# A decoder layer on one core: some transposes moved from TensorE to DMA, and element work shifted between VectorE, ScalarE and GpSimd

## What is computed

```python
x = x + attn(layernorm(x))     # 16 query heads in 4 groups, 4 key heads, rope, causal softmax, y @ Wo + bo
x = x + xattn(layernorm(x), ctx, mask)   # scores = x @ ctx.T / 16, masked softmax, readout = attn @ ctx
x = x + ffn(layernorm(x))

def ffn(x):                    # I = 704
    xq, w1q = q(x), q(w_gate_up)         # q: v / (max|v| / 127) rounded to integers, times the scale, per row
    gate, up = split(xq @ w1q.T, I)
    hq, w2q = q(silu(gate) * up), q(w_down)
    return hq @ w2q.T
```

## Time and profile before

| | us |
|---|---|
| Median of three runs | 102.81 |
| The three runs | 101.42, 102.81, 103.00 |
| The profiled execution, its own time | 101.47 |
| Its span, first to last instruction | 99.80 |
| Outside the span | 1.67 |
| Busy in the span: PE, DVE, POOL, ACT | 90.2, 75.7, 66.1, 65.7 |

### The profile page before, as it was taken

The page is one execution under the profiler, slowest core; times in us unless marked ns, Lnnn a source line. Parts: engine busy times, 40 slices in busy tenths (PEclk is TensorE's granted clock), DMA queues, the critical chain, the costliest instruction groups (busy, mean ns, idle before and its releaser), DMA issues.

```text
span 99.8 us, 2432 instructions
## 1 busy us (share of the span) xinstructions
PE 90.2 (90%) x804; PEld 68.8 (69%) x804; DVE 75.7 (76%) x217; ACT 65.7 (66%) x175; POOL 66.1 (66%) x136
## 2 busy tenths in 40 slices
PE   5999699999889999989999999979999999999560
PEld 4698467977576676767776777768778887775220
DVE  5046979957998988877896659797977788988731
ACT  1404216938839886776597878969986996988410
POOL 6266847975787977914638788848868962892220
PEclk9999999999999999999999999999999999999995
DMA  2999999940000000000000000000000010012121
GB/s 36 346 337 415 419 407 409 360 143 3 3 0 7 0 3 0 7 0 0 0 7 0 0 0 0 3 7 0 0 0 0 0 56 7 0 59 99 55 103 53
DMA packets 4521, 8.34 MB, mean 84 GB/s; under 512 B 349, under 2 KB 3358, under 8 KB 4382
## 3 DMA queue, kind: packets, MB, share of 16 engines
q1 hardware_dynamic: 4272, 7.96, 21.7%
q10 hardware_dynamic: 238, 0.23, 0.9%
HBM read 7.15 MB, written 1.05 MB: 82 GB/s over the span
## 4 chain that ended last, share of the span: by engine, by line
PE 72%; DVE 10%; POOL 7%; issue 5%; ACT 3%; DVEq 0%; POOLq 0%; ACTq 0%
PE ps_s L443 14%; PE ps_r L262 6%; PE ps_q L303 6%; PE ps_y L525 4%; PE ps_r L289 4%; PE ps_r L386 3%; PE ps_x L375 3%; PE ps_s L339 3%; PE ps_y L351 3%; PE ps_y L359 3%; PE ps_q L311 2%; PE ps_x L365 2%; DVE rot L846 2%; PE ps_s L469 2%; PE ps_y L354 2%
## 5 line engine op out<-in xcount | busy, mean ns | idle before, releaser
L1156 POOL TENSOR_TENSOR gate_up<-gate,up_row 128x704 f32<-128x704 f32 x7 | 11.9, 1698 | 3.7 <-ACT gate L723 3.5
L262 PE MATMUL ps_r<-warm 128*128 128x256 bf16 x60 | 9.4, 317 | 1.1 <-DVE warm L771 1.1
L262 PEld LDWEIGHTS ps_r<-warm 128*128 128x128 bf16 x60 | 6.7, 115 | 3.0 <-DVE warm L771 1.1
L1125 POOL TENSOR_TENSOR rot_c<-rot,b_rope 128x128 f32<-128x128 f32 x8 | 3.7, 459 | 7.5 <-DVE rot L846 7.5
L869 DVE RECIPROCAL y_rsum<-ps_y 128x128 f32<-128x128 f32 x8 | 7.6, 951 | 1.1 <-PE ps_y L354 1.0
L443 PE MATMUL ps_s<-gate_hi,x_int_T 128*128 128x352 f32 x28 | 7.5, 350 | 0.0
L1187 POOL TENSOR_TENSOR y_out<-ffn,x_aug 128x256 f32<-128x256 f32 x7 | 5.1, 729 | 3.7 <-DVE ffn L1025 3.7
L525 PE MATMUL ps_y<-w_T,h_T 128*128 128x256 bf16 (+1 forms) x42 | 6.5, 276 | 0.9 <-DVE ffn L1025 0.8
L443 PE MATMUL ps_s<-up_int,x_int_T 128*128 128x352 f32 x32 | 6.9, 337 | 0.0
L443 PE MATMUL ps_s<-gate_lo,x_int_T 128*128 128x352 f32 x28 | 6.8, 323 | 0.0
L610 ACT ACTIVATE p_self_T<-ps_s 128x512 f32<-128x512 f32 x8 | 4.8, 597 | 2.4 <-PE ps_s L339 2.4
(11 more groups left out here) (194 smaller groups left out, 285.8 us busy)
## 6 DMA issues: line engine op xcount, KB each, us to landing
ctxT<-in_ctxT SPq DMA_DIRECT2D x1, 1024.0 KB, 8.6
w_raw<-in_w SPq DMA_DIRECT2D x2, 512.0 KB, 11.0
ctx_aug<-in_ctx SPq DMA_DIRECT2D x1, 1024.0 KB, 17.0
out_x<-y_out SPq DMA_DIRECT2D x8, 128.0 KB, 1.7
x_aug<-in_x SPq DMA_DIRECT2D x1, 768.0 KB, 6.8
xT<-in_xT SPq DMA_DIRECT2D x1, 768.0 KB, 9.8
w_raw<-in_w SPq DMA_DIRECT2D x1, 704.0 KB, 14.6
x_first<-in_x_first SPq DMA_DIRECT2D x1, 416.0 KB, 4.3
```

The lines of the kernel that those rows point to most:

```text
L262: nc.tensor.matmul(ps_r[:, 0:2 * T], warm[:, 0:P], warm[:, :], start=True, stop=True)
L1156: nc.gpsimd.tensor_tensor(gate_up[j % 2][:, :, :], gate[j % 2][:, :, :], up_row[:, :].rearrange("p (i f) -> p i f", i=2), ALU.mult).then_i ...
```

## The change

- The up half of w1 (int16), w2 and h of batches 0 to 5 are transposed by DMAs from SP's queue, from SBUF to SBUF. For w2 and h, DVE first copies the int16 values to bf16 (`widen_w2`, `widen_h`) into buffers of 768 columns laid over w1_raw. The PE transposes and evacuations for them are gone; up_int is still written by ACT, now from up_T in SBUF. h of batches 6 and 7 goes through PE as before.
- The row scales of w1 and w2 are transposed once on PE (13 rows), copied, stored to DRAM by one DMA and read back into all partitions by a second; up_row and w2_row are views of the result.
- `scale_down` of batches 0 to 5: ACT multiplies by h_scale (`scale_down_rows`), then POOL multiplies by w2_row (`weigh_down`). Batches 6 and 7 stay on DVE.
- `rotate_sum` moves from DVE to POOL, all eight batches, same operation.
- EARLY = 3: batch 2 takes tanh too.
- The lists of all engines are written anew. PE's list has 61 keep_warm matmuls. SP's queue holds, behind the loads: the up transpose, the scale store and reload, two w2 transposes, then the transposes of h and the stores as listed.

The diff, cut (the removed helpers are those named above):

```diff
+    BY_DMA = 6
+    SPLIT = 6
...
-    EARLY = 2
+    EARLY = 3
...
+        w1_flat = w1_raw[:, :, :].rearrange("p o d -> p (o d)")
+        UT = (WT - GT) * DC * P // 2
+        up_T = w1_flat[:, 0:UT].bitcast(I16).rearrange("p (o c t) -> p o c t", c=DC, t=P)
+        padded = w1_flat[:, UT:UT + 2 * FC * P].bitcast(BF16).rearrange("p (i f) -> p i f", f=FC * P)
+        w2_bf = padded[:, 0:DC]
+        h_bf = [padded[:, DC + i] for i in range(2)]
...
+            done(sp, "w1_int_ready", 4)
+            sp.dma_start_transpose(up_T[:, :, :, :].rearrange("p o c t -> p (o c) t"),
+                                   w1_int[:, GT:WT, :].rearrange("p o d -> p (o d)")).then_inc(s["up_T_loaded"], 16)
+            done(sp, "scale_rows_ready", 0)
+            sp.dma_start(scale_rows_dram, scale_rows[:, :]).then_inc(s["scale_rows_stored"], 16)
+            sp.wait_ge(s["scale_rows_stored"], 16)
+            sp.dma_start(out_rows[:, :], scale_rows_dram.rearrange("o p -> (o p)")[FF:2 * FF + D].unsqueeze(0).to_broadcast([P, FF + D])).then_inc(s["rows_loaded"], 16)
+            done(sp, "pads_zero", 0)
+            for c in range(DC):
+                done(sp, "w2_bf_ready", c)
+                sp.dma_start_transpose(w2_T[:, :, c * P:(c + 1) * P], w2_bf[:, c, :]).then_inc(s[f"w2_T_{c}_loaded"], 16)
+
+            def transpose_h(j):
+
+                done(sp, "h_bf_ready", j)
+                if j >= 2:
+                    done(sp, "down_done", j - 2)
+                sp.dma_start_transpose(h_T[j % 2][:, :, :], h_bf[j % 2]).then_inc(s[f"h_T_{j}_loaded"], 16)
...
+            transpose_h(0)
+            transpose_h(1)
+            transpose_h(2)
+            transpose_h(3)
+            transpose_h(4)
+            store_out(0)
+            transpose_h(5)
+            store_out(1)
+            store_out(2)
...
+                nc.tensor.transpose(ps_r[0:WT + DC, 0:P], w_scale[:, :], ident[:, :]).then_inc(s["scales_transposed"], 1)
...
+                    for c in range(DC):
+                        pe.wait_ge(s[f"w2_T_{c}_loaded"], 16)
+                if j >= 1 and j - 1 < SPLIT:
+                    done(pe, "down_scaled", j - 1)
+                elif j >= 1:
+                    done(pe, "ffn_ready", j - 1 - SPLIT)
+                if j < BY_DMA:
+                    pe.wait_ge(s[f"h_T_{j}_loaded"], 16)
+                else:
+                    done(pe, "h_T_ready", j - BY_DMA)
...
+            readout(4, "x2_ready", 3); cross_scores(5); gate_product(0); project_out(6)
+            transpose_x_int(3, "x2_ready", 4); transpose_cross_p(5); weigh_values(7)
+            readout(5, "x_int_T_ready", 3); up_product(0); transpose_x1(6); gate_product(1); cross_scores(6)
+            transpose_x_int(4, "x2_ready", 5); project_out(7); up_product(1); gate_product(2)
+            transpose_cross_p(6); transpose_x1(7); readout(6, "x_int_T_ready", 4); cross_scores(7)
+            gate_product(3); up_product(2); transpose_x_int(5, "x2_ready", 6); transpose_cross_p(7)
+            up_product(3); gate_product(4); readout(7, "x_int_T_ready", 5); down(0); gate_product(5)
+            transpose_x_int(6, "x2_ready", 7); up_product(4); down(1); gate_product(6); up_product(5)
+            transpose_x_int(7, "x_int_T_ready", 6); down(2); up_product(6); last_gate(0); down(3); last_gate(1)
+            up_product(7); down(4); transpose_h(6); down(5); down(6); last_transpose_h_a(); last_transpose_h_b()
+            last_down_a(); last_down_b()
...
+            def evacuate_up(c):
+
+                act.wait_ge(s["up_T_loaded"], 16)
+                nc.scalar.copy(up_int[:, c, 0:FL], up_T[:, 0, c, FL:P])
+                nc.scalar.copy(up_int[:, c, FL:FF].rearrange("p (o t) -> p o t", t=P), up_T[:, 1:WT - GT, c, :]).then_inc(s["up_int_ready"], 1)
...
+            def scale_down_rows(j):
+
+                free(act, "y_out_ready", j, 3)
+                done(act, "down_done", j)
+                nc.scalar.mul(ffn[j % 3][:, :], ps_y[:, 0:D], h_scale[:, j:j + 1]).then_inc(s["down_scaled"], 1)
...
+            quantise_h(0); square_2(6); exp_cross(7); silu_gate(3); quantise_h(1); evacuate_x_int(5)
+            evacuate_cross_p(7); silu_gate(4); quantise_x(6); quantise_h(2); scale_down_rows(0)
+            evacuate_x_int(6); silu_gate(5); quantise_h(3); scale_down_rows(1); quantise_x(7); silu_gate(6)
+            quantise_h(4); square_2(7); evacuate_x_int(7); scale_down_rows(2); quantise_h(5); scale_down_rows(3)
+            last_silu(0); last_silu(1); quantise_h(6); scale_down_rows(4); evacuate_h(6); scale_down_rows(5)
+            last_quantise_h(0); last_quantise_h(1); last_evacuate_h_a()
...
+                nc.vector.tensor_copy(w2_bf[:, c, 0:FF], w2_int[:, c, :]).then_inc(s["w2_bf_ready"], 1)
...
+            def widen_h(j):
+
+                if j >= 2:
+                    dve.wait_ge(s[f"h_T_{j - 2}_loaded"], 16)
+                done(dve, "h_int_ready", j)
+                nc.vector.tensor_copy(h_bf[j % 2][:, 0:FF], h_int[j % 2][:, :]).then_inc(s["h_bf_ready"], 1)
...
+            amax_x(4); step_x(4); invert_x(4); invert_cross_sum(5); residual_1(6); finish_gate(0)
+            invert_sums(7); residual_2(5); normalise_y(7); amax_x(5); hidden(0); step_x(5); invert_x(5)
+            max_cross(6); finish_gate(1); bias_cross(6); residual_1(7); amax_h(0); invert_cross_sum(6)
+            scale_h(0); invert_h(0); hidden(1); finish_gate(2); residual_2(6); max_cross(7); bias_cross(7)
+            widen_h(0); amax_h(1); invert_cross_sum(7); hidden(2); scale_h(1); invert_h(1); amax_x(6); amax_h(2)
+            step_x(6); invert_x(6); widen_h(1); scale_h(2); invert_h(2); hidden(3); residual_2(7); amax_h(3)
+            amax_x(7); widen_h(2); scale_h(3); invert_h(3); hidden(4); step_x(7); invert_x(7); amax_h(4)
+            widen_h(3); scale_h(4); invert_h(4); hidden(5); amax_h(5); widen_h(4); scale_h(5); invert_h(5)
+            hidden(6); widen_h(5); amax_h(6); scale_h(6); invert_h(6); last_widen(0); last_widen(1)
+            last_hidden(0); last_hidden(1); last_amax_h(0); last_amax_h(1)
+            last_scale_h(); scale_h(7); invert_h(7); scale_down(6); last_evacuate_h_b(); scale_down(7)
+            add_residual(7)
...
+            def weigh_down(j):
+
+                done(pool, "down_scaled", j)
+                nc.gpsimd.tensor_tensor(ffn[j % 3][:, :], ffn[j % 3][:, :], w2_row, ALU.mult).then_inc(s["ffn_weighed"], 1)
...
+                if j < SPLIT:
+                    done(pool, "ffn_weighed", j)
+                else:
+                    done(pool, "ffn_ready", j - SPLIT)
...
+            rstd_1(0, 1, 1); scale_rope(0); sum_bias(); rope_bias(); rotate_c(0); rotate_sum(0); rstd_1(1, 2, 2)
+            scale_rope(1); centre_x(0); centre_x(1); rotate_c(1); rotate_sum(1); rstd_1(2, B, 3); centre_x(2)
...
+            scale_x(0); rstd_2(2); rotate_c(6); rotate_sum(6); drop_later_keys(4); whole_x2(1); scale_x(1)
+            rstd_2(3); drop_later_keys(5); rotate_c(7); rotate_sum(7); rstd_2(4); drop_later_keys(6)
+            whole_x2(2); scale_x(2); whole_x2(3); rstd_2(5); whole_x2(4); drop_later_keys(7); widen_gate(0)
+            scale_x(3); rstd_2(6); widen_gate(1); rstd_2(7); scale_x(4); widen_gate(2); whole_x2(5); scale_x(5)
+            widen_gate(3); widen_gate(4); scale_x(6); widen_gate(5); whole_x2(6); weigh_down(0); widen_gate(6)
+            add_residual(0); scale_x(7); weigh_down(1); add_residual(1); weigh_down(2); weigh_down(3)
+            add_residual(2); weigh_down(4); add_residual(3); weigh_down(5); add_residual(4); whole_x2(7)
+            add_residual(5); add_residual(6)
```

## The result

The changed kernel takes 98.95 us (median of five, 98.59 to 101.78) beside 101.42 us for the kernel before (101.11 to 103.0): the ratio is 0.976, 95% interval 0.972 to 0.980. That is 2.5 us less, inside the range of 94.3 to 101.8 and inside the forecast's own band of 96 to 99.5. The gain is smaller than forecast all the same: 97.6 against 102.81, the median known then, was 5.2 us. Of it 1.3 was that median above the profiled 101.47, and 0.4 went off for scatter; the sum of the stretches had 4.3.

What follows compares the result with a forecast made beforehand. It took PE as the bound until 89.43 us, then a serial chain. gate_product(0) at 56.35 plus 39.2 gave 95.55; 1.67 outside the span made 97.2, and 0.4 for scatter 97.6 us; range 94.3 to 101.8.

Steps and rivals of the forecast that it cites:

- PE's waits on qk_rot: Ahead of transpose_qk: PE idle on qk_rot of over 2 us in sum would show the prediction wrong, rotate_sum queued on POOL.
- The rival of slow transfers: Transfers of h decide from 3.5 us each, costing 0.7 up to 4.2, then two for one; 105.9 at 8 us; chance 0.13.
- transposes that do not relieve PE: Each transpose moved to DMA is matched by waiting, as with transfers of about 5.5 us: 100.9; no chance of its own.
- The rival of PE as the only bound: Whole kernel: POOL costs nothing and PE stays the bound, 94.2 us, 94.6 with scatter; chance 0.16 (below 96).
- PE's stall ahead of up_product(3): Middle phase: PE reaches up_product(3) at 12.9 and stands 1.4 us, since gate_up(2) is ready at 13.3 and hidden(2) at 14.3.
- Before gate_product(0): Front: PE saves 1.75 us net, 0.65 lost to rotate_sum in POOL's queue (bounds 0 and 2.7); gate_product(0) starts at 56.35.
- The widening on DVE: DVE's int16 to bf16 copies of 704 elements: 0.35 us each, bounds 0.27 and 0.54.
- Middle phase: From the start of gate_product(0) to the end of up_product(7): 27.6 us, PE's 26.2 plus a stall of 1.4, against 31.97.
- The room of the transfers: From widen_h(5) done at 26.8 to down(5) due by 30.3: 3.5 us, so a transfer of 3.0 costs nothing.
- the prediction's rule: Transfers of h: no cost to 3.5 us, 0.7 up to 4.2, then each further us costs two; 2.9 at 5.3.
- End: After up_product(7): POOL's queue ends at 36.7 with add_residual(6), DVE's last y_out at 35.6; issue and store give 39.2.
- The ring of three ffn buffers: Near the end: ties scale_down_rows(5) on ACT, ahead of last_quantise_h, to add_residual(2) at 31.3; claimed just not late.

Runs made afterwards that it cites:

- h_pe: The changed kernel with h of all batches transposed on PE and evacuated by ACT, no widening or transposing DMA for h; 102.13 us, ratio 1.003 to before.
- rot_dve: The changed kernel with rotate_sum of all eight batches put back on DVE; 99.17 us, ratio 0.973 to before.
- hid_first: The changed kernel with amax_h(1) and hidden(2) ahead of widen_h(0) in DVE's list; 99.75 us, ratio 0.967 to before.
- widen_act: The changed kernel with the widening copy of h on ACT, behind quantise_h, in place of DVE; 99.49 us, ratio 0.979 to before.
- split0: The changed kernel with the down scaling of all batches on DVE, none split over ACT and POOL; 102.86 us, ratio 0.998 to before.
- twice: The changed kernel with each transposing transfer of h issued twice, first into an unread area, both waited for; 104.43 us, ratio 1.027 to before.
- early2: The changed kernel with silu by tanh for two batches only, batch 2 taking silu behind the table load; 105.72 us, too scattered for a ratio.
- rot_hid: The changed kernel with rotate_sum back on DVE and hidden(2) ahead of widen_h(0) together; 98.68 us, ratio 0.968 to before.
- w2late: The changed kernel with maximum, scale, inverse, quantising and widening of W2 moved later, behind residual_1(0); 100.5 us, ratio 0.989 to before.
- bench: The changed kernel with a tail behind its last result, timing DVE copies, a scale and maxima with POOL idle or busy; executed once, 109.02 us.
- pad_front: The changed kernel with sixteen unread warm matmuls added to PE ahead of gate_product(0), four at each readout of batches 1 to 4; 100.71 us, ratio 0.989.
- front_order: The changed kernel with the lists' order ahead of gate_product(0) put back as in the kernel before, every edit kept; 103.63 us, ratio 1.013 to before.

## Why the prediction was right or wrong

**Right.** The sign, and the range. PE's work: 1.75 and 4.7 us forecast, 1.83 and 4.5 measured (31.18 to 26.64 in the middle's own limits). POOL at 75. The transfer of h at 3.0 for 2.7. POOL's list from gate_product(0) on: gate_up(2) ready at 13.3 forecast, 13.2 measured, and add_residual(6) done at 36.7 forecast and measured. PE's waits on qk_rot stayed under the 2 us that were named as a sign of being wrong (1.5). The rival of slow transfers is excluded by 2.7 us and by h_pe, that of transposes that do not relieve PE by h_pe too. The rival of PE as the only bound falls by its idle time of 2.8 in the middle.

**Right by luck.** PE's stall ahead of up_product(3) was forecast at 1.4 and measured 1.50, but not for the forecast's reason. gate_up(2) of POOL came on time; hidden(2) ended at 15.1 after the start of gate_product(0) and not at 14.3, mostly because of the held copy, and PE came to up_product(3) at 13.7 and not at 12.9. Two delays of 0.8 cancelled. Without the copy the stall is 0.86, and that is the order of PE's own list. The whole also gains by errors of opposite sign: front and middle gave 2.7 less than forecast, and the end cost 0.7 less.

**"Before gate_product(0)" failed.** It had 0.65 of 1.75 lost, to rotate_sum in POOL's queue. All but 0.1 were. rot_dve gives back 0.8, near the 0.65, but in it the scale of W2 is no longer held (0.30 us in place of 1.43) and PE's wait for x1 is gone, so the 0.8 holds both the queue, which the prediction priced, and the hold on DVE, which it did not; the two were not separated. The other 0.9 is there with rotate_sum on DVE too. The largest new wait in rot_dve is 1.01 for the mask of batch 0, which the new order of PE's list no longer covers with mean_ctx; no run takes it away alone. So the step that failed is twofold: POOL's own additions were priced, and not what a POOL without a pause does to DVE's instructions, and the new order of the front was put at nothing.

**The widening on DVE was mis-sized.** It was taken at 0.35 with 0.54 as the upper bound. Alone it is 0.34, so the estimate of the copy was right and its upper bound wrong: the copy beside POOL took up to 1.37, 0.67 in the mean. The nearest row had its source in PSUM, and nothing in the prediction asked who was running beside it. What it cost in time is not shown: with the longest copy out of the way (hid_first) the middle stays as it is.

**"Middle phase" failed by 1.5.** It had 27.6 for 29.08, from PE's 26.2 and one stall of 1.4. PE's work is right, and the size of that stall. The further 1.3 us of idle time are smaller waits, each 0.2 to 0.4, on p_cross_T, x1, h_T and hid, and gaps that no row names; the sum had none of them. Taking the long copy off DVE (widen_act) or out of the way (hid_first) lowers the one stall to 0.86 and leaves the phase at 29.5 or more, because the transfer of h of batch 0 (hid_first) or ScalarE (widen_act) is next. The table has 29.5 in seven kernels, but five of them, after among them, repeat the same lists there, stall included. That is no sign of a common limit. What would shorten the phase was not found.

**The room of the transfers was wrong.** "Room: 3.5 us, 3.0 costs nothing" counted the distance of two batches at the end. At 2.7 PE already waits 0.2 us twice, and 4.05 cost 5.5 us where the prediction's rule gave 0.6. The rule also left out the clock, and that transpose_h(5) stands behind a store in SP's queue: it took 3.2 us in after and 4.3 to 4.6 in four other profiles, the others 2.7.

**"End" was too dear by 0.6, and by the wrong path.** 11.6 forecast, 11.05 measured. The sum let POOL's queue end the kernel at 36.7 after the start of gate_product(0), 1.1 behind DVE's last y_out at 35.6. POOL did end there, but DVE's last y_out came at 37.6 and the store followed it. h_inv(7) was ready at 33.6 and not 31.5, with the middle 1.5 late and 0.9 of wait for GpSimd in the last_widen halves, which the sum did not have; from h_inv(7) on it took the forecast 4.05. The ring of three ffn buffers, forecast as just not late, was late: scale_down_rows(5) waited 0.53 for add_residual(2), and PE 0.84 for ScalarE behind it.

**The clock was not in the sum at all.** In the profiled execution of after it did no harm (1.00 in front and middle, six matmuls of a down product in 0.92 to 0.93 to the end). But another of the five executions has a granted clock of 0.946 and took 101.78, no less than before. In split0, twice and early2 a PE stall of 2 to 3.5 us was followed by 1.2 GHz; in hid_first the waits at the end are those of after (0.24 and 0.82 for 0.23 and 0.84), and yet the granted clock of its end is 0.67 and six matmuls took 1.45. So the stalls alone do not tell when it falls.

No kernel tried is clearly faster than the changed one; rot_hid may be.

## What to carry to other kernels

When work is moved to GpSimd, price what it does to VectorE too: list VectorE's copies, scales and two-source products that would run beside it, and take as the upper bound of each that it waits until GpSimd next pauses; one GpSimd instruction is the least to count. Work taken from the bounding engine is a gain only as far as the idle time of that engine stays as it was, so write its idle time down before and after, stage by stage, and look at what the work taken away had covered: two steps that depend on each other need other work between them. A transfer that lands just in time has no room: double it once and look.

## What was not expected of the hardware

- Some VectorE instructions end only with the GpSimd instruction beside them, or with the third or fourth of a row without a pause (1.43 in after, 1.79 in w2late): a copy of 704 int16 to bf16 took 1.80 for 0.34 us, a scale of 128x2 took 1.63, a product of 128x8 took 1.79; a maximum of 704 took 0.89 either way.
- A transposing DMA of h landed in 2.7 to 3.3 us mostly, but the sixth, issued right behind the store of batch 0, took 4.6 in w2late, 4.5 in bench, 4.4 in pad_front and 4.3 in early2; in the first three its issue took 2.07 to 2.36 us in place of 1.21, and in all four PE stood for 1.62 to 1.85 us ahead of the down product. The store behind the transfer in SP's queue was not tried.
- 30 matmuls at the start of the program took 5.04 to 6.23 us from one execution to the next, which alone makes over 1 us of scatter.
- After a PE stall of 2.05 us (split0), 3.45 (early2) or 2.83 (twice) the granted clock of the following stretch was 0.50 to 0.63, and six matmuls of a down product took 1.55 to 1.57 us in place of 0.92. In hid_first the clock fell at the end with no wait above 0.82 before it, in front_order to 0.83 after waits of 1.22, 1.06 and 1.50.
